# A graph-attention kernel on one core: slot order of the flags products, and an earlier way into the main slots

## What is computed

```python
row_zero = v.sum(-1) == 0
q_exp = where(row_zero[..., None], 0, q[:, None, :])
self_feat = concat([v, q_exp]) @ W_self.T + b_self
output = self_feat
for d in range(2):
    A = adj if d == 0 else swapaxes(adj, 1, 2);  A = A[:, :, :20]
    mask, label_bias = A.sum(-1) > 0, A @ w_bias + b_bias
    kv = self_feat[:, :20]                       # 20 keys per batch
    aff = q_h . k_h / sqrt(32)                   # 16 heads of 32
    w = softmax(where(mask, aff, NEG) + label_bias)
    output = output + (w @ kv) @ Wout[d] + bout[d]
return v + relu(output)
```

## Time and profile before

| | us |
|---|---|
| median of 3 runs (lowest, highest) | 1803.17 (1800.65, 1807.22) |
| the profiled execution's own time | 1803.32 |
| its span from first to last instruction | 1800.7 |
| PE busy / weight loads busy | 1760.4 / 1595.1 |
| DVE / ACT / POOL busy | 1113.4 / 947.5 / 777.2 |

### The profile page before, as it was taken

The page is one execution under the profiler, slowest core; times in us unless marked ns, Lnnn a source line. Parts: engine busy times, 40 slices in busy tenths (PEclk is TensorE's granted clock), DMA queues, the critical chain, the costliest instruction groups (busy, mean ns, idle before and its releaser), DMA issues.

```text
span 1800.7 us, 44640 instructions
## 1 busy us (share of the span) xinstructions
PE 1760.4 (98%) x14472; PEld 1595.1 (89%) x14472; DVE 1113.4 (62%) x1812; ACT 947.5 (53%) x1655; POOL 777.2 (43%) x691
## 2 busy tenths in 40 slices
PE   8999999979999999999999999999999999999997
PEld 5899999968988988888888889988888888998885
DVE  2667776866666666666666666666666666666532
ACT  2344444445555555555555555555555555555543
POOL 0444443214444444444444444444444444444444
PEclk9999999979999999999999999999999999999998
DMA  6133334466656554655555556556564655556421
GB/s 212 47 85 85 92 103 111 122 150 168 169 145 171 150 170 135 172 153 155 154 155 157 161 149 188 152 156 169 151 172 143 164 156 155 153 155 182 129 79 57
DMA packets 291516, 258.07 MB, mean 143 GB/s; under 512 B 105968, under 2 KB 221936, under 8 KB 291312
## 3 DMA queue, kind: packets, MB, share of 16 engines
q1 hardware_dynamic: 277920, 244.97, 48.8%
q10 hardware_dynamic: 13392, 10.51, 1.8%
HBM read 199.25 MB, written 56.10 MB: 142 GB/s over the span
## 4 chain that ended last, share of the span: by engine, by line
PE 91%; SPq 2%; issue 2%; DMA 2%; DVE 1%; ACT 1%; POOL 1%; POOLq 0%; ACTq 0%; DVEq 0%
PE bank L1664 29%; PE bank L1678 20%; PE low_banks L939 10%; PE low_banks L1638 9%; PE bank L1699 9%; PE bank L939 5%; PE bank L1691 4%; PE bank L1658 2%; PE bank L486 2%; SPq L1354 1%; PE bank L1706 1%; PE low_banks L462 0%; DMA stage<-in_L_cond_Wq 0%; SPq L658 0%; PE bank L502 0%
## 5 line engine op out<-in xcount | busy, mean ns | idle before, releaser
L1664 PE MATMUL bank<-kx,xt_main 128*128 128x160 f32 x4096 | 599.9, 300 | 0.0
L1664 PEld LDWEIGHTS bank<-kx,xt_main 128*128 128x128 f32 x4096 | 575.8, 191 | 3.0
L1504 POOL TENSOR_TENSOR res<-res,xk 128x512 f32<-128x512 f32 x128 | 163.7, 1279 | 451.5 <-ACT res L1543 451.5
L1561 ACT ACTIVATE wtt<-bank 128x384 f32<-128x384 f32 (+1 forms) x256 | 109.8, 429 | 432.5 <-PE bank L1691 432.5
L1397 DVE TENSOR_TENSOR sc<-bank,masks 128x320 f32<-128x320 f32 x256 | 125.7, 491 | 328.2 <-PE bank L1664 326.2
L1548 ACT ACTIVATE kx<-low_banks 128x1920 f32<-128x1920 f32 (+5 forms) x201 | 306.3, 1524 | 37.4 <-PE low_banks L1638 37.3
L1486 POOL TENSOR_TENSOR sc<-sc,mx 128x640 f32<-128x640 f32 x128 | 160.1, 1272 | 301.5 <-DVE mx L1409 301.5
L1678 PE MATMUL bank<-ws_h,xh_main 128*128 128x512 f32 x512 | 222.1, 434 | 3.5 <-DVE res L1423 3.4
L1638 PE MATMUL low_banks<-key_tile,a_rows 32*128 32x160 f32 (+3 forms) x4288 | 202.8, 315 | 6.4 <-ACT kx L1548 5.8
L1678 PE MATMUL bank<-ws_h,xl_main 128*128 128x512 f32 x512 | 204.7, 400 | 0.0
L1678 PE MATMUL bank<-ws_l,xh_main 128*128 128x512 f32 x512 | 203.2, 397 | 0.0
(11 more groups left out here) (146 smaller groups left out, 2937.6 us busy)
## 6 DMA issues: line engine op xcount, KB each, us to landing
rows_main<-in_x SPq DMA_DIRECT2D x256, 128.0 KB, 3.7
xs<-in_x SPq DMA_DIRECT2D x64, 512.0 KB, 4.7
xk<-in_x SPq DMA_DIRECT2D x64, 512.0 KB, 3.7
res<-c_dram SPq DMA_DIRECT2D x64, 512.0 KB, 5.4
out<-res SPq DMA_DIRECT2D x128, 256.0 KB, 3.4
adj<-in_mask_BxSxSx_ik SPq DMA_DIRECT2D x32, 440.0 KB, 5.3
adj<-in_mask_BxSxSx_ik SPq DMA_DIRECT2D x128, 110.0 KB
vbd<-v_dram SPq DMA_DIRECT2D x768, 10.0 KB
```

Of the source, the lines that this page charges most:

```text
L1504: pool.tensor_tensor(res[:, p.par, b, :], res[:, p.par, b, :], xk[:, p.par, b, :], ALU.add).then_inc(res_ready, 1)
L1664: mm = nc.tensor.matmul(dst, xt[:, j, p.ring + b, :], kx[:, t.par, :, 2 * j:2 * j + 2, w * NG:w * NG + NG] .rearrange("p r c m -> p c r m" ...
```

## The change

On **PE in the slots** each flags product is split from its scores (`open_bank`). In a full slot the order is: open age 3, open age 2, scores age 3, turn (late, 1, 0), scores age 2, turn (late, 1, 1), generate 0, values (late, 1), flag row of t itself, open age 1, scores age 1, generate 1, all 12 self products (soft, 0), open age 0, turn (soft, 0, 0), scores age 0 of batch 0, turn (soft, 0, 1), mask, generate 2, values (soft, 0), scores age 0 of batch 1, self products (soft, 1). `flags_out` on ACT moves up behind the exponentials. In **strip rounds** the slots with a narrow window (the first three and the last three) take 8 units or 4 units a round in place of 3. The **last scored slot** has an order of its own and a second output bank. In the **keys-and-values stage** POOL adds the four chunks of x, and one fp32 product with ones takes the place of 8. In its last two halves constants, edges, `xs` and flags of the first pairs are made and loaded sooner. `mk` is dropped and its values are written over `cn`.

```diff
@@ keys_and_values, sync_program
             elif not last:
                 sp.wait_ge(x_turned, C * HALVES)
...
                 v["early_loads"](sp)
-            if last:
                 sp.wait_ge(pe_feat, C * HALVES)
                 sp.wait_ge(f_low, C * HALVES)
                 v["late_loads"](sp)
             for m in range(NK):
+                if last and m == NK - 1:
+                    v["first_constants"](sp)
                 sp.wait_ge(v_turned, NK * n + m + 1)
...
+                if last and m == 3:
+                    store_constants(n)
@@ vector_program
-            if last:
-                v["early_mask"](dve)
             for m in range(NK):
...
+                if last and m == 3:
+                    turn_constants(n)
+                if last and m == 4:
+                    v["early_weights"](dve)
+                if last and m == 5:
+                    v["early_mask"](dve)
+            if last:
+                v["early_flags"](dve)
@@ gpsimd_program
+        def add_chunks(n, par):
+            pool.wait_ge(x_turned, C * n + C)
+            if due(n):
+                pool.wait_ge(pe_sum, n)
+            for j in range(1, C):
...
+                pool.tensor_tensor(chunk_sum[:], x_cols(xt, 0, par) if j == 1 else chunk_sum[:], x_cols(xt, j, par),
+                                   ALU.add).then_inc(chunks_added, 1)
@@ scalar_program
-                if m == 5:
+                if m == (2 if last else 5):
                     constants_high(n)
+            if tail and not last:
+                v["early_sums"](act)
@@ tensor_program, sums
-            for j in range(C):
-                for k, part in enumerate((xh, xl)):
-                    mm = nc.tensor.matmul(slot_bank(1 - par, SUM_SLOT), ones[:], x_cols(part, j, par),
-                                          start=(j == 0 and k == 0), stop=(j == C - 1 and k == 1))
+            nc.tensor.matmul(slot_bank(1 - par, SUM_SLOT), ones[:].bitcast(F32), chunk_sum[:],
+                             start=True, stop=True).then_inc(pe_sum, 1)
@@ window_loop
+    def early_flags(dve):
+        dve.wait_ge(set_once, 3)
+        nonzero_rows(dve, Pair(0, 0))
+        count_and_weigh(dve, 0, 1)
+        total_and_mask(dve, 0, 1)
+    def first_constants(sp):
+        sp.wait_ge(v["z_stored"], 16 * 2 * NQ * 2 * v["KBLOCKS"])
+        sp.wait_ge(zc_cleared, 1)
+        load_constants(sp, Pair(0, 0))
@@ rounds
+            if hi - lo == 2:
+                return (tuple(range(2 * C)),)
+            if hi - lo < WIN:
+                return (tuple(range(C)), tuple(range(C, 2 * C)))
@@ scalar_program, slot
                 exponentials(soft, 1)
+            if t.real():
+                flags_out(t)
             if late.real():
                 clip(late, 1)
@@ self_features
+            if closing(p):
+                if b == 0:
+                    pe.wait_ge(s_added, 4 * PAIRS - 1)
+                else:
+                    pe.wait_ge(out_taken, n - 1)
+            elif due(n):
+                pe.wait_ge(out_taken, n)
@@ tensor_program
+        def last_scored(t):
+            soft, late = t.back(3), t.back(4)
+            open_bank(t, 3)
+            scores(t, 3)
+            self_features(soft, 0)
+            turn_weights(late, 1, 0)
+            turn_weights(late, 1, 1)
+            values(late, 1)
+            self_features(soft, 1)
+            turn_weights(soft, 0, 0)
+            turn_weights(soft, 0, 1)
+            values(soft, 0)
```

More of the change, by code:

```diff
@@ L820, in one_half @@
             if not tail:
+                add_chunks(n + 2, par)
                 x_lows(n + 2, par)
+            elif not last:
+                pool.wait_ge(pe_feat, C * HALVES)
+                v["early_clear"](pool)
             constants_low(n)
+        add_chunks(0, 0)
         conditions(0)
@@ L826, in gpsimd_program @@
             feature_low(0, 0, j)
+        add_chunks(1, 1)
         pool.wait_ge(v["cq_out"], 2 * NK)
@@ L1105, in window_loop, with closing, out_bank @@
     NR = len(ROUNDS)
+    def closing(p):
+        return isinstance(p.k, int) and p.n == PAIRS - 1
+    def out_bank(p, b):
+        return bank[5 - AGES * PAIRS % 2] if closing(p) and b == 0 else OUT
     class Pair:
@@ L1139, in window, with rounds, gone, round_at @@
         return min(ws), max(ws) + 2
-    def generated(g, lo, hi):
-        n = len(ROUNDS[g])
-        return low_banks[:, :, 0:n * UN].rearrange("p r (u x) -> p r u x", u=n)[:, :, :, lo * NG:hi * NG]
-    def taken(t, g, lo, hi):
-        return kx[:, t.par, :, ROUNDS[g][0]:ROUNDS[g][-1] + 1, lo * NG:hi * NG]
+    def rounds(t):
+        if isinstance(t.k, int):
+            lo, hi = window(t)
+            if hi - lo == 2:
+                return (tuple(range(2 * C)),)
+            if hi - lo < WIN:
+                return (tuple(range(C)), tuple(range(C, 2 * C)))
+        return ROUNDS
+    def gone(t):
+        if isinstance(t.k, int):
+            return sum(len(rounds(Pair(u // 4, u % 4))) for u in range(min(t.n, PAIRS + AGES - 1)))
+        return NR * t.n - 4
+    def round_at(t, place):
+        n = len(rounds(t))
+        return {1: (0, None, None), 2: (0, None, 1), 3: (0, 1, 2)}[n][place]
+    def generated(t, g):
+        lo, hi = window(t)
+        n, w = len(rounds(t)[g]), (hi - lo) * NG
+        return low_banks[:, :, 0:n * w].rearrange("p r (u x) -> p r u x", u=n)
+    def taken(t, g):
+        lo, hi = window(t)
+        r = rounds(t)[g]
+        return kx[:, t.par, :, r[0]:r[-1] + 1, lo * NG:hi * NG]
     def unit(t):
@@ L1319, in slot @@
                     sp.wait_ge(pe_s, scored(t.back(1), 3))
-                elif t.n < 2:
-                    sp.wait_ge(zc_cleared, t.n + 1)
-                load_constants(sp, t)
+                elif t.n == 1:
+                    sp.wait_ge(zc_cleared, 2)
+                if not (isinstance(t.k, int) and t.n == 0):
+                    load_constants(sp, t)
             if has_window(n) and due(t.n + 1):
-                sp.wait_ge(pe_gen, NR * (t.n + 1))
+                sp.wait_ge(pe_gen, gone(t.back(-1)))
                 load_keys(sp, n)
@@ L1562, in weights_out @@
                                  ACT.Copy).then_inc(wtt_ready, 1)
-        def row_sums(p):
-            act.wait_ge(xs_loaded, 16 * p.n + 16)
-            if p.back(1).real():
-                act.wait_ge(nz_ready, 2 * p.n)
-            for b in range(2):
-                nc.scalar.activation(xs[:, b, :], xs[:, b, :], ACT.Copy, accum_out=sums[:, b:b + 1]).then_inc(summed, 1)
         def flags_out(p):
@@ L1579, in place_masks @@
             act.wait_ge(m_done[0], t.half + 1)
-            act.wait_ge(pe_gen, NR * (t.n + 1) + NR)
+            act.wait_ge(pe_gen, gone(t.back(-2)))
             for d, m in enumerate((m0s[:], MASK.rearrange("p (b m) -> p b m", b=EDGE))):
@@ L1605, in slot @@
                 scale_condition(soft, 1)
-            if nxt.real():
-                row_sums(nxt)
+            if nxt.real() and not (isinstance(nxt.k, int) and nxt.n == 0):
+                row_sums(act, nxt)
             if has_window(nxt):
@@ L1657, in scores @@
                 pe.wait_ge(s_added, n - 2)
-            nc.tensor.matmul(s_bank(t, a).rearrange("p (b x) -> p b x", b=2), flags[:, p.c % AGES, :], zu,
-                             start=True, stop=False)
-            for b in range(2):
+            nc.tensor.matmul(s_bank(t, a).rearrange("p (b x) -> p b x", b=2), flags[:, p.c % AGES, :],
+                             zc[:, p.c % AGES, :, o * NQ * NG:(o + 2) * NQ * NG], start=True, stop=False)
+        def scores(t, a, batches=(0, 1)):
+            p = t.back(a)
+            if a == ages(t)[0]:
+                pe.wait_ge(gen_taken, gone(t.back(-1)))
+            if a == 0:
+                pe.wait_ge(x_turned, C * (p.n + 1))
+            for b in batches:
                 w = 2 * (AGES - 1 - a) + b
@@ L1736, in slot @@
             if soft.real():
-                self_features(soft, 0, range(0, 2))
+                self_features(soft, 0)
+            if t.real():
+                open_bank(t, 0)
+            if soft.real():
                 turn_weights(soft, 0, 0)
-                self_features(soft, 0, range(2, C))
+                if t.real():
+                    scores(t, 0, (0,))
                 turn_weights(soft, 0, 1)
+            if t.n == 0:
+                scores(t, 0)
             if t.c % 2 == 0 and t.real():
```

164 lines of the change are left out of this document (94 added, 70 removed).

## The result

The changed kernel takes 1809.48 us (median of 11 runs, 1807.45 to 1814.88), the kernel before 1802.93 beside it (11 runs, 1799.46 to 1807.22). The ratio is 1.0038 with an interval of 1.0027 to 1.005: 6.5 us slower, within the 0.5% that I had called no change. The forecast of 1804.4 was 5 us too low, the range of 1789 to 1814 held the time. The profiled execution took 1810.98 us, its span 1809.2. (In one later session one of 23 executions of the kernel before took 4376 us; it is counted slow and is in no ratio here.)

A forecast was written before the change was run, and what follows sets the result against it. PE, busy 499.52 of 500 us, was taken to bound full slots, with a hidden wait for ACT's copy. Slots +14.7, sums -5.0, way in -4.5, end -4.0 give +1.2 on 1803.3; less 0.15, 1804.4 us, range 1789 to 1814.

The forecast's parts named there:

- Opening of age 2: Full slots: moved ahead of scores age 3, the flags product adds 0.15 us a slot, +9.2 us for about 61 slots.
- Flag row: Full slots: costs 0.10 us behind values, old place gives back 0.05; net +0.05 a slot, +3.0 us in 61 slots.
- Bank of outputs and junction: Full slots: self products (soft, 1) wait 0.06 us for DVE's emptying, +3.7; uncut self products save 0.02 a slot, -1.2.
- Rivals three and four: Full slots: three, DVE empties the output bank late, 1816.5 us; four, moved turn parts lose 0.2 us margin; together chance 0.13.
- Sums: Keys-and-values stage: one fp32 product for 8 saves 0.63 us on PE in each of 8 halves, -5.0 us.
- Way in: From last half into slots: sooner constants, wide rounds; slot 1 starts 3 us sooner; -4.5 us (bounds -10 and 0).
- no longer late: Way in: said of the constants, which were not last to arrive in most of that stretch; late next is `xs`.
- End: Last slots: last scored slot's chain to last values 19.6 us for 24.1; -4 us in all (bounds -7 and -1).
- slots 64 and 65: End: lose 0.9 us each, with nothing between their turn parts, and gain about 1.5 in rounds.
- half clock that may come again: End: part of the rest of the gain was work at half clock, which might return; no size of its own.
- a landing of 3.2 us: Way in: skill's fit for 512 KB, where the row has 6.3; by it 2.5 us more gain at each such wait.
- Rival two: Way in: `xs` lands in 4.7 us, not 6.3, at three waits, no half clock; gains 10 us, 1799; chance 0.12.

## Why the prediction was right, and where it was wrong

- **Opening of age 2: right.** +0.15 a slot was the forecast, 0.147 was measured by taking it back and 8.1 us in all by adding it alone. The distance of 0.14 us between copy and values, and the same distance behind a booked wait in slot 65, were the whole evidence, with no idle time booked in full slots; it held.
- **Flag row: mis-sized.** +0.05 a slot was taken, +0.097 measured. The new place costs 0.11 for the 0.10 taken; the old one gives back 0.02 and not 0.05. By the Trainium skill's formula for the gap of one product ("TensorE: Matmul & The Clock Gate", "Back-to-back issue gap"), which the section gives for an isolated product, it would have been 0.056 in the new place; the row shows 0.11.
- **Bank of outputs and junction: right as a net.** 0.06 - 0.02 = 0.04 a slot forecast, 0.04 measured; but the wait for DVE is 0.04 and the uncut run saves nothing (+0.01), so that it fits to the digit is luck. Rivals three and four didn't come: no wait for DVE long enough to be booked shows in the full slots, and turn parts keep their cover.
- **Sums: right**, -5.0 forecast, -5.2 in the profiles counted from the first of these products, -5.6 by the ratio alone.
- **Way in: the step that failed.** The prediction had pair 1's `xs` issued at 369 and landed at 375, so 2.4 and 2.0 us later than before, or 9.1 and 15.1 behind the start of the last projection; it was 12.1 and 16.75. I let half of the moved transfers' 4.8 us vanish in gaps of SP's list; where DVE's scaling was short, the issue still came 3.6 to 4.0 us later than before in four traces of five (2.9 in the fifth), and the scaling added 1.5 where it was long, which I had not in the sum at all. I also took one landing time for all, and it is 4.6 to 8.0 us. The list of waits ended at slot 1 besides; behind it, pair 1's constants came late in the trace of after, which I had called "no longer late", and pair 0's are still waited for. Instead of -4.5 the stretch gave +2.0 in the one profile, -1.7 on average over the traces, and by the timed ratios (-1.6 for way in and end, of which the end is some -2.6) about +1, with 3.4 us either way: small, and its sign stays open.
- **End: right in kind, off in size.** -4 forecast, -2.4 in the profile of after. The chain to the last values of the last scored slot was right: 19.6 us forecast for 24.1, and 1802.53 - 1783.02 = 19.5 measured, at full clock. The term that failed is slots 64 and 65: they were to lose 1.8 and win 1.5 back by wide rounds, and they take 40.4 us for 38.2, 2.2 more (38.4 with the old slot order). The prediction's "half clock that may come again" came with `zc` in pieces.

Two smaller things in the prediction don't hold: a landing of 3.2 us in place of 6.3 would win 3.1 us at each wait by its own numbers, not 2.5; and its zero of 360.8 is the start of the generation behind the last projection, 0.9 us later than the zero used here.

So the sum is, in the profiles, 13.5 (+15.3 without the odd stall) - 4.7 + 2.0 - 2.4 = 8.4 in place of 14.7 - 5.0 - 4.5 - 4.0 = 1.2. The direction of every part held but that of the way in, which is not settled. Way in and end, taken at -8.5 and measured at -1.6 by time, are more than the 5 us by which the forecast was low; that the time fell into the range is owed to the slots and the sums, which carry most of it. Rival two, a way in that gains 10 us because transfers land in 4.7, did not come: pair 1's `xs` did land in 4.6 us (367.38 to 372.01), but was issued too late, and pair 2's took 8.3 (373.37 to 381.68).

## What to carry to other kernels

When a consumer starts within one semaphore's time (0.15 us here) behind its producer in every period, take it for waiting, even where the trace books no idle time: here, work moved out of that stretch to its front cost its full length. When transfers are moved ahead of others on a queue, count each at its issue time (0.37 to 0.40 us for a small store, 0.75 for a load of constants here) against the first thing behind that is waited for, ask what the issuing engine itself waits for in between, and go on to the second and third such thing. And undo a combined change part by part: the sums alone, and the whole change without its slot order, beat the kernel before, while two reorderings of a few products turned it into a loss. Compare a stretch of one profile with the same stretch of the others before reading 2 us into it: here the full slots repeated within 1 us, while the way in moved by up to 5 and the end by 3 between kernels alike there.

## What the runs showed of the hardware that I had not expected

DVE's scaling of a 128x80 tile waits out POOL's clearing of another tile. DVE and POOL, kernel after, in order of time:

```profile
356.73 1.17 POOL L1560 MEMSET zc<- 128x1280 f32 x1 [5.03 <-ACT kv_vst L918]
357.01 4.17 DVE L1328 TENSOR_SCALAR cn<-cn 128x80 f32<-128x80 f32 x1
357.83 3.30 POOL L1561 MEMSET zc<- 128x3840 f32 x1
```

It ends at 361.18, just behind the second clearing at 361.13, and so it does in five more traces; elsewhere the same instruction takes 0.19 to 0.21 us. With `zc` cleared in pieces of some 0.6 us it takes 0.40. In two traces it got in between the two clearings, as in that of the old slot order, where the first one ends at 359.40:

```profile
358.51 0.94 DVE L1328 TENSOR_SCALAR cn<-cn 128x80 f32<-128x80 f32 x1
```

In the kernel before, the same two kinds met as well: 1.55 us for a 128x2 scaling at 363.66, in a clearing that ended at 365.19. DVE's TENSOR_REDUCE beside a clearing kept its time (1.61 us at 363.81, as elsewhere). This agrees with the Trainium skill, "SBUF — State Buffer", section "Who interferes with whom", by which such a scaling can take the port pair that it shares with POOL, and whoever comes second is blocked for the whole instruction; that it can be held out by two in a row, the runs show. It cost SP 1.7 us and pair 1's `xs` 1.5, but no time that the runs could tell (1.0036 with the pieces, 1.0038 without).
